# Feed-forward weights through a ring of column pairs, shared down products turned round, downs two columns behind

## What is computed

```
x = x + attn(cond(x, ...))
h = cond2(x, ...)                                   # mixer: scans, gates, layer norm
dispatch = order[:, :320]                           # per expert, its first 320 tokens
eout   = (silu(xg @ rg) * (xg @ ru)) @ rd           # 8 experts, 256 -> 1024 -> 256
shared = (silu(h @ sg) * (h @ su)) @ sd             # 256 -> 2048 -> 256
x = x + shared + sum_of_experts(eout * weight)
```

## Time and profile before

| | us |
|---|---|
| median of 3 runs (lowest, highest) | 1663.79 (1660.51, 1671.43) |
| the profiled execution, whole | 1664.96 |
| its span, first to last instruction | 1663.2 |
| attention part, to the first `gu` | about 1024.8 |
| chunks 0 to 2 with mixer and router | 1024.8 to 1341.8 |
| experts | 1343.97 to 1574.5 |
| chunk 3 | 1574.4 to 1658.9 |
| PE busy over the span | 1557.2 (94%) |
| DVE, ACT, POOL busy | 52%, 44%, 42% |
| mean granted PE clock | 0.955 of full |

### The profile page before, as it was taken

The page is one execution under the profiler, slowest core; times in us unless marked ns, Lnnn a source line. Parts: engine busy times, 40 slices in busy tenths (PEclk is TensorE's granted clock), DMA queues, the critical chain, the costliest instruction groups (busy, mean ns, idle before and its releaser), DMA issues. The chain is left out here.

```text
span 1663.2 us, 20499 instructions
## 1 busy us (share of the span) xinstructions
PE 1557.2 (94%) x7136; PEld 747.0 (45%) x7136; DVE 870.3 (52%) x2297; ACT 734.2 (44%) x998; POOL 696.3 (42%) x516
## 2 busy tenths in 40 slices
PE   5699999989999999898999898999999999999998
PEld 3423333323333333332333233555656577777755
DVE  7578878888677865556765723343422111111141
ACT  4754666765566655475545466233211111111111
POOL 4437999987799998153210121400000200000070
PEclk9659999999999999999998888999999999999999
DMA  3551033233231320344432015100040005243071
GB/s 96 145 154 32 23 83 74 74 93 78 65 84 33 78 46 14 73 118 108 124 74 64 28 34 166 61 0 0 0 152 4 23 0 184 92 157 119 16 129 23
DMA packets 76178, 121.39 MB, mean 73 GB/s; under 512 B 15192, under 2 KB 53537, under 8 KB 73003
## 3 DMA queue, kind: packets, MB, share of 16 engines
q1 hardware_dynamic: 72155, 113.62, 24.5%
q0 software_dynamic: 3072, 6.03, 2.1%
q10 hardware_dynamic: 848, 0.43, 0.1%
HBM read 85.05 MB, written 36.96 MB: 73 GB/s over the span
## 5 line engine op out<-in xcount | busy, mean ns | idle before, releaser
L1145 POOL TENSOR_TENSOR sb_prob<-sb_prob,sb_weight 128x1024 f32<-128x1024 f32 x192 | 448.4, 2371 | 44.6 <-ACT sb_prob L1361 44.1
L1361 ACT ACTIVATE sb_prob<-wide 128x1024 f32<-128x1024 f32 (+3 forms) x384 | 347.1, 916 | 210.7 <-PE wide L1974 107.4
L1969 PE MATMUL wide<-sb_stack_q,sb_stack_k 99*128 99x512 bf16 (+3 forms) x896 | 285.7, 369 | 17.4 <-ACT sb_prob L1361 7.5
L1656 DVE CUSTOM_DVE_ANT_0 sb_junk<-bank,sb_bias 128x512 bf16<-128x512 f32 x339 | 226.7, 687 | 61.4 <-PE bank L1944 56.3
L1405 ACT ACTIVATE sb_sil<-wide 128x320 f32<-128x320 f32 (+1 forms) x128 | 66.2, 517 | 436.0 <-PE wide L2048 436.0
L1944 PE MATMUL bank<-sb_stack_k,sb_stack_q 96*128 96x512 bf16 (+3 forms) x597 | 217.6, 383 | 20.0 <-DVE sb_rowmax L1656 5.4
L2048 PE MATMUL wide<-sb_weight,sb_ffn 128*128 128x512 f32 x512 | 233.2, 599 | 0.0
L1989 PE MATMUL wide<-sb_prob,sb_v_aug 128*17 128x512 f32 (+3 forms) x1792 | 225.3, 569 | 7.7 <-ACT sb_o_raw L1374 6.0
L1783 DVE TENSOR_TENSOR sb_act_s<-sb_sil,wide 128x512 f32<-128x512 f32 x64 | 43.9, 687 | 255.0 <-ACT sb_sil L1405 255.0
L1183 POOL DMA_INDIRECT sb_weight<-slots_out,sb_slot_r x32 | 31.5, 986 | 283.9 <-issue 282.1
L2048 PE MATMUL wide<-sb_xgT,sb_big 128*128 128x320 f32 x512 | 147.0, 433 | 1.4 <-ACT sb_xgT L1420 1.4
(11 more groups left out here) (272 smaller groups left out, 1827.9 us busy)
## 6 DMA issues: line engine op xcount, KB each, us to landing
sb_stack_k<-parts SPq DMA_DIRECT2D x32, 256.0 KB, 6.8
o_raw<-sb_o_raw SPq DMA_DIRECT2D x32, 256.0 KB, 2.3
sb_big<-rg SPq DMA_DIRECT2D x8, 1024.0 KB, 4.9
sb_big<-ru SPq DMA_DIRECT2D x8, 1024.0 KB, 7.3
sb_big<-rd SPq DMA_DIRECT2D x8, 1024.0 KB, 10.6
sb_stack_q<-parts SPq DMA_DIRECT2D x16, 384.0 KB, 5.1
parts<-sb_o_norm SPq DMA_DIRECT2D x40, 128.0 KB
sb_stack_q<-parts SPq DMA_DIRECT2D x16, 256.0 KB, 5.6
```

Source lines behind the costliest of these rows:

```text
L1145: e.tensor_tensor(p, p, weight_of(*u[1:]), ALU.mult).then_inc(weigh_p.handle, 1)
L1361: e.activation(p[:, :, first:HALF], sc[:, :, first:HALF], ACT.Exp).then_inc(SC.empty_sem(u), 1)
L1656: e.tensor_tensor_reduce(out=junk[:, i % 2, 0:hi - lo], in0=BK.tile(u)[:, 0:hi - lo], in1=bias[:, qt, lo:hi], scale=1.0, scalar=-3e38, op0 ...
L1969: i = e.matmul(sc[:, j * HALF + first:(j + 1) * HALF], stack_k[0:ROWS_M, n % 3, g, kt * P:(kt + 1) * P], stack_q[0:ROWS_M, n % 3, g, half ...
```

## The change

1. Weights: one ring of 12 pieces in SBUF (`RAWS`), each for a pair of columns, shared or expert, in the order of use (`COLUMNS`, 64 pairs). A piece is 3 transfers of 256 KB with rows of 1 KB. The shared weights are loaded again for every chunk. Pairs 0 and 1 are loaded behind the attention (`ffnload`), 2 to 11 at its end, and pair p as `wload` behind the `down` that ends pair p-12. `eload` is gone.
2. Shared `down`: the weight slice is now stationary and 512 tokens stream past, 2 matmuls for 4. The sum is then channels by tokens; `total_T` (DVE, two halves) adds it to xT in place, and `yT` (PE, two units of 4 transposes a chunk) turns it, ACT copies it to `y`. `resT` is gone.
3. `down` of column i-2 follows `gu` of column i (`LAG`), across the borders of chunks and experts too. silu and product share one ring of 3 tiles.
4. `send` is one unit a token tile; the `resid` units stand one step earlier; the mixer's tiles of batch row 1 overlap more in `big`. `fetch` of expert x+1 still stands behind the fourth column of expert x, on all engines; on SP it now also waits for the mixer's end.

```diff
+LAG, ACTS = 2, 3
+COLUMNS = [("s", tc, i) for tc in range(CHUNKS - 1) for i in range(COLUMNS_S)]
+COLUMNS += [("e", x, i) for x in range(E) for i in range(COLUMNS_R)]
+COLUMNS += [("s", CHUNKS - 1, i) for i in range(COLUMNS_S)]
+N_PAIRS, EARLY, RAWS = len(COLUMNS) // 2, 2, 12
...
+def columns_of_chunk(plan, kind, x, others, late):
+
+    n = COLUMNS_S if kind == "s" else COLUMNS_R
+    for i in range(n):
+        k = COLUMNS.index((kind, x, i))
+        plan.append(("gu", kind, x, i))
+        if k >= LAG:
+            ended(plan, k - LAG)
+        plan += late.pop(i, [])
...
+def ended(plan, k):
+
+    of_, x, i = COLUMNS[k]
+    plan.append(("down", of_, x, i))
+    if k % 2 and k // 2 + RAWS < N_PAIRS:
+        plan.append(("wload", k // 2 + RAWS))
+    if of_ == "s" and i == COLUMNS_S - 1:
+        plan.append(("total_T", x))
+    if of_ == "e" and i == COLUMNS_R - 1:
+        plan.append(("eout", x))
...
     for x in range(E):
-        for i in range(COLUMNS_R):
-            plan.append(("gu", "e", x, i))
-            if i:
-                plan.append(("down", "e", x, i - 1))
-            if i == 3 and x + 1 < E:
-                plan.append(("fetch", x + 1))
-        plan.append(("down", "e", x, COLUMNS_R - 1))
-        if x + 2 < E:
-            plan.append(("eload", x + 2))
-        plan.append(("eout", x))
...
+        late = turned(2) if x == 0 else {}
+        if x + 1 < E:
+            late[3] = late.get(3, []) + [("fetch", x + 1)]
+        columns_of_chunk(plan, "e", x, [], late)
...
+            def load_pair(p):
+                kind, x, i = column_pair(p)[0]
+                g, u, d = ([A["sg"], A["su"], A["sd"]] if kind == "s" else [A["rg"][x], A["ru"][x], A["rd"][x]])
+                if p >= RAWS:
+                    w.wait_ge(down_done(*column_pair(p - RAWS)[1]))
+                sig, piece = w_in[p % RAWS].handle, w_raw(p)
+                for z, src in enumerate((g, u)):
+                    e.dma_start(piece[:, z * DC * 2 * P:(z + 1) * DC * 2 * P].rearrange("p (c m) -> p c m", c=DC),
+                                chunks(src)[:, :, i * P:(i + 2) * P]).then_inc(sig, 16)
+                e.dma_start(piece[:, 2 * DC * 2 * P:].rearrange("p (j n) -> p j n", j=2),
+                            chunks(d)[:, i:i + 2]).then_inc(sig, 16)
...
             for mark in attention_done:
                 w.wait_ge(mark)
-            for k in range(EARLY, BLOCKS):
-                load_block(k)
+            for p in range(EARLY, RAWS):
+                load_pair(p)
...
+                        for c in range(DC):
+                            m = e.matmul(acc[:, c * HALF:(c + 1) * HALF], down_rows(w_raw(p), j)[:, c * P:(c + 1) * P], a,
+                                         start=(i == 0), stop=final, skip_group_check=True)
```

More of the change, by code:

```diff
@@ L438, in attention_plan, with column_pair, sends, beside @@
     return first_plan() + with_splits(flat(plan), SPLIT_AT)
+def column_pair(p):
+    return COLUMNS[2 * p:2 * p + 2]
 def route_plan(b):
[L442 to L448, removed]
-        if i:
-            plan.append(("down", "s", tc, i - 1))
+    return [("logit", b), ("soft", b), ("pick", b)] + [PAUSE] * (4 * b) + [("pos", b), ("slots", b)]
+def sends(b):
+    return [("send", b, t) for t in range(b * NT, (b + 1) * NT)]
+def beside(units, others):
+    out = []
+    for k, u in enumerate(others):
+        out.append(u)
+        if k % 2 and units:
+            out[-1] = [units.pop(0)] + flat([u])
+    return out + units
+def columns_of_chunk(plan, kind, x, others, late):
[6 more added lines that the diff above has]
+        plan += late.pop(i, [])
         for _ in range(STEPS_PER_COLUMN):
@@ L453, in shared_plan, with turned @@
                 plan += flat([others.pop(0)])
-    return plan + [("resT", tc), ("down", "s", tc, COLUMNS_S - 1)]
+def ended(plan, k):
[7 more added lines that the diff above has]
+        plan.append(("eout", x))
+def turned(tc):
+    return {LAG + 1: [("yT", tc, 0), ("yT", tc, 1)]}
@@ L474, in tail_plan @@
-    tiles = [(t, k) for t in range(B * NT) for k in range(TOPK)]
+    others = [("num", *last), *route[:3], ("inv", *last), *route[3:5], ("times", *last), PAUSE]
+    mixer = mix_plan(1)
+    others += beside(sends(0), [outputs(1, 1)[k:k + NH] for k in (0, NH)] + mixer)
+    plan = []
+    columns_of_chunk(plan, "s", 0, others, {})
+    columns_of_chunk(plan, "s", 1, others, turned(0))
+    plan += flat(others) + [("pad",)]
+    columns_of_chunk(plan, "s", 2, route_plan(1) + sends(1), turned(1))
@@ L481, in tail_plan @@
+    plan += flat(others)
+    for k in range(LAG):
+        ended(plan, len(COLUMNS) - LAG + k)
+    plan += [("yT", CHUNKS - 1, 0), ("yT", CHUNKS - 1, 1)]
     return plan + [("total", t) for t in range(last, B * NT, 2)]
@@ L528, in tail_uses @@
             for u in TAIL:
-                if u[0] in (*MIXED, "resid", "logit", "pos"):
+                if u[0] in (*MIXED, "resid", "logit", "pos", "yT"):
                     keys.append(u)
@@ L676, in s2, with w_raw, gate_up, down_rows @@
             return sb(name, shape, dt, ph2)
[L678 to L683, removed]
+        pieces, at = {}, 0
+        for a, n, name in sorted((a, PAIR_W, ("raw", k)) for k, a in enumerate(RAW_AT)):
+            if a > at:
+                s2(f"gap{a}", [P, a - at])
+            pieces[name] = s2("_".join(str(z) for z in name), [P, n])
+            at = a + n
+        def w_raw(p):
+            return pieces["raw", p % RAWS][:]
+        def gate_up(piece, z, c, j):
+            return piece[:, (z * DC + c) * 2 * P + j * P:(z * DC + c) * 2 * P + (j + 1) * P]
+        def down_rows(piece, j):
+            return piece[:, 2 * DC * 2 * P + j * D:2 * DC * 2 * P + (j + 1) * D]
         best_f = s2("best_f", [P, B * NT, TOPK])
@@ L2076, in _ @@
+                    m.then_inc((acc_done if final else down_done_p).handle, 1)
+                elif kind == "yT":
+                    _, tc, k = u
+                    w.wait_ge(ACC.emptied(("acc", "s", tc)) if k else half_T.after(("total_T", tc)))
+                    w.wait_ge(BT.vacant(u))
+                    for t in range(2):
+                        at = tc * HALF + (2 * k + t) * P
                         for c in range(DC):
-                            m = e.matmul(acc[:, t * D + c * P:t * D + (c + 1) * P],
-                                         xT[:, c, tc * HALF + t * P:tc * HALF + (t + 1) * P], F["ident"], start=False,
-                                         stop=False, skip_group_check=True)
+                            m = e.transpose(BT.tile(u)[:, t * D + c * P:t * D + (c + 1) * P], xT[:, c, at:at + P], F["ident"])
+                    m.then_inc(BT.full_sem(u), 1)
```

192 lines of the change are left out of this document (78 added, 114 removed).

## The result

The changed kernel is slower: 1756.23 us (median; 1754.01 to 1759.49) against 1667.49 us (1660.51 to 1671.43) for the kernel before on the same chip, a ratio of 1.0543, 95% interval 1.0515 to 1.0571. The prediction was 1720, range 1700 to 1745: the sign and the main mechanism were right, the size was not, and one cost stood nowhere in it.

The account below looks back on a forecast made before the run. The prediction took PE to bound the tail. Terms of +36.4, +12, +10, -3.6 and +1.6 summed to +56.4 us on the profiled 1664.96, 1721.4; that execution was 1.2 us over the median, so 1720 us, range 1700 to 1745.

Parts of the forecast that it names:

- waits for tokens: At eight expert starts, PE waits about 5.1 us for the tokens' load; less the old 3.5 us, +36.4 us.
- half speed after them: In the experts, PE runs at half clock after each of eight token waits, 1.5 us each: +12 us, bounds 0 and 24.
- expert products, third tile: Expert `down`: the operand's shrinking from 128 to 64 columns doesn't shorten the 256 that stream; no time taken.
- last division, with its clock: At the attention's end, PE idles 8.4 us behind late denominators, plus 1.5 for the clock: +10 us, bounds 3.9 and 14.
- turned sums: In four chunks, `yT` transposes replace `resT` at half its PE time, 0.89 us less each: -3.6 us.
- end: After the last `down`, two halves of `total_T`, a `yT` unit and the second sum follow: about +1.6 us.
- weights, mixer: PE waits on the weight stream: nothing taken; mixer starting earlier: nothing taken, up to 3 us kept for the range.
- Rival 1: In the tail, the token waits are there but the clock holds: 1706.5 us, chance 0.16.

Follow-up runs that it names:

- e1: Changed kernel with the third token tile's stationary operand in the expert `down` 128 columns wide again instead of 64: 1739.0 us, ratio 1.0430.
- e2: Changed kernel with the tokens' load issued earlier on SP, behind the first column of the expert before instead of the fourth: 1689.04 us, ratio 1.0145.
- e6: Changed kernel with the tokens' load issued ahead of the pair load on SP, behind the same `down`: 1721.38 us, ratio 1.0340.
- e4: Changed kernel with a 128-column third tile, tokens loaded earlier on SP, and the last division ahead of the late pairs: 1657.76 us, ratio 0.9943.
- e8: e4 with the downs one column behind (`LAG = 1`) instead of two: 1658.5 us, ratio 0.9961 to the kernel before.
- e5: Kernel before the change, with only the third token tile's stationary operand in the expert `down` 64 columns wide instead of 128: 1682.26 us, ratio 1.0112.
- e7: Changed kernel with the third token tile's stationary operand in the expert `down` 96 columns wide instead of 64: 1739.97 us, ratio 1.0469.

## Where the prediction was right, and which step failed

The tail grew by 93.5 us. By the prediction's own steps:

| step | predicted | measured | from |
|---|---|---|---|
| waits for tokens | +36.4 | +44.5 | 48.0 - 3.5 |
| half speed after them | +12 | +17.4 | 29.2 - 8 x 2.15 in `gu`, 12.3 - 6.9 in the transposes |
| expert products, third tile | 0 | +20.4 | 64 `down` x 0.14, 57 `gu` x 0.20 (7 are followed by a wait); e1 gave 14 to 17 back |
| last division, with its clock | +10 | +14.6 | 10.5 + 1.9 - 0.2 waits, `resid` 9.4 us for 7.0 |
| turned sums | -3.6 | -3.4 | 7.8 us (`resT`) to 4.4 (`yT`) |
| end | +1.6 | +1.5 | 5.8 for 4.3 us behind the last `down` |
| weights, mixer | 0 | 0 | no such wait |
| sum | +56.4 | +95.0 | less 1.7 us of old waits on ACT and DVE: 93.3, the tail's +93.5 |

**The step that failed** is the sentence on the third tile, "shrinks from 128 to 64 columns, which doesn't shorten the 256 that stream". It asked only whether the edit could gain. The runs showed 20.4 us in its place, more than half of the 37 us by which the tail grew beyond the forecast. I costed the edit by its streamed columns, as I did the turned `down`, where that held (120.9 us before, 120.0 after). Every expert matmul of the kernel before had the full width, but its trace did hold the price, in a product of the mixer with 64 columns (L1841; first its row by form, then the chain around it):

```profile
L1841 PE MATMUL bank<-sb_xT,sb_weight 128*64 128x512 f32 x8 | 3.6, 598 | 0.0
...
1068.27 3.43 PE wide L2048 x8
...
1073.43 3.58 PE bank L1841 x8
1077.00 3.63 PE wide L2048 x8
```

The `gu` behind it takes 3.63 us, the one at 1068.27 and that of the earlier trace rows 3.43: the same 0.20 us. The mixer, also taken at zero, got up to 3 us of bounds; this term got none.

With this term the forecast had been 1740; with the three mis-sized terms right and this one at nothing, 1738. Both lie inside the range, the two together don't.

**The waits** were the right mechanism, in the right eight places, with the right chain: SP's three weight issues took 1.44 us as read off and the first tokens' issue 0.51 (0.63 taken), and e2 removes waits and clock without touching PE's order. The landing was mis-sized: I took 2.7 us behind the second issue (4.8 in all, less SP's 2.07), and 4.1 was measured: I let half of the pair be through before the tokens joined. By the rows of single microseconds the queue was fuller than that: SP's first issue began at 1409.34, bytes moved only after 1410 (my estimate had about 1 us for this), and by the second tokens' issue at 1411.29 some 0.2 MB of the pair's 0.79 were through. The whole 1.1 MB took until after 1414, not 3.1 us, at 65 to 346 GB/s by those rows, and the load landed 0.30 us behind the last microsecond with traffic. e6 separates the parts: with nothing ahead of it the load lands in 2.6 us and the wait is 3.0. So of the 6.0 us, 3.0 are SP's order and the queue, 3.0 the late release.

**The clock** fell as the rows of before foretold, after all eight waits. The price was 2.2 us each instead of 1.5. That a part of the half speed falls into the idle time was right: over the eight waits the mean granted clock was 0.85, 0.72, 0.94, 0.74, 0.90, 0.71, 0.89 and 0.69, and since the slices show only 1.00 and 0.50, 0.7 to 4.0 us of each wait stood at 0.50 already. Where much of it did, little of the work was slow: the first `gu` took 4.27 us behind the wait at 0.94 and 2.89 behind the one at 0.69. What was short is the half speed left for the work, about 4.4 us on average instead of 3. Rival 1, that the clock holds, is out for waits of 6 us; e6 shows it true for four of eight waits of 3 us. What tells those four from the others stays open.

**The division**: both waits came, 1.9 us at `pos` (forecast 1.7) and 10.5 at `resid` (6.7). From the reciprocal to the end of `times` took 12.6 us (forecast 12.7). What was short is the time to the denominators: 27.9 us from the first weight issue to the reciprocal instead of 24, because their own eight issues (3.88 us) begin only when the thirtieth weight issue is out. That the attention ended 4.4 us earlier in this execution moved both sides alike: PE came to `resid` at 1051.6 instead of 1056.0, and SP began its issues at 1021.55 instead of 1025.98. The slow work behind the wait cost 2.4 us instead of 1.5.

**What stays open.** Between the tails, e4 is faster than the kernel before by 2.7 us (635.7 against 638.4), which the terms left over explain to within 2 us: -3.4 for the turned sums, -3.5 and -1.7 for old waits, +1.5 at the end, +2.4 of waits at `pos` and `resid`. The medians differ by more, 10 us in e4's comparison and 7 in e8's. In the two profiled executions 7.0 us separate the kernels, and the other 4.3 lie in the attention. Its end moved between 1018.9 and 1028.6 in these profiles (1022.8 and 1024.8 with the attention of the kernel before); no run here was made to find out whether the change has a part in that.

## What to carry to other kernels

Cost every edit that changes an operand's shape as if it could lose, and look for a matmul of the new shape in the trace you have: a ragged last tile that is "only smaller" can be dearer than a full one, and padding it to full width was worth nearly 1% here. When a load and its user are put behind the same event, ask what the user's engine does in between; a transfer's release belongs a few columns ahead of its use. Its place in the issuing queue made half of each wait here (e6). A wait of PE has to be priced with the half-speed work after it, here about a third on top, of waits of 6 us (17.4 on 48.0) and of 3 us (7.7 on 23.7) alike.

## What the runs showed of the hardware that was not expected

- A matmul with a 64-column stationary operand between full-width ones costs time on both sides: 0.34 us a column of this kernel, 16.6 us by the medians over 64 columns in e5. 96 columns cost nothing that the rows show (e7).
- Waits of about the same length are not followed by the same clock: of eight of 3.0 us, four left it at full speed and four did not (e6).
- The clock can fall inside the wait: it stood at 0.50 for 0.7 to 4.0 us of each wait of the changed kernel (4.8 to 6.4 us), and the more it did, the shorter was the slow work behind it.
- The tokens' second transfer (64 KB, 0.4 us behind the first) took 2.6 us from issue to landing with nothing else ahead of it, and 4.1 us behind 0.79 MB of weights issued just before.
